# The third batch's mix as seven half products, and an attention stage laid out call by call

## The reference, cut to what matters

```python
# four batches of x [512 rows, 512 columns]; context [512 rows, 256]
q = ctx @ Wq.T + bq;  k = ctx @ Wk.T + bk
attention = softmax(q @ k.T)                      # 512 x 512
x = x + tanh(g_xattn) * (layernorm(x) @ attention.T)   # "the mix", 512 x 512 x 512
h = layernorm(x)
up, gate = h @ ternary(W_up).T, h @ ternary(W_gate).T  # 2048 columns each
x = x + tanh(g_ffn) * ((silu(up) * gate) @ ternary(W_down).T)
# ternary(w) = clip(round(w / scale), -1, 1) * scale, scale = mean(|w|)
```

## Time and profile before

| What | Value |
|---|---|
| median of three runs | 391.25 us |
| the profiled execution | 390.47 us |
| its span, first to last instruction | 388.6 us |
| tensor engine busy | 384.4 us, 99% of the span |
| VectorE, ScalarE, POOL busy | 315.8, 271.0, 196.5 us |
| attention stage on the tensor engine | until 91.28 us |
| granted clock | 1.00 in each of 40 slices |

### The profile page before, as it was taken

How to read it: one execution, slowest core, us unless ns; L and a number is a source line. 1 busy time by engine, 2 the same in 40 slices (tenths; PEclk the granted TensorE clock), 3 DMA queues, 4 the chain that set the end, 5 groups by cost and what they waited for, 6 DMA issues and landing times.

```text
span 388.6 us, 6367 instructions
## 1 busy us (share of the span) xinstructions
PE 384.4 (99%) x2043; PEld 223.9 (58%) x2048; DVE 315.8 (81%) x495; ACT 271.0 (70%) x372; POOL 196.5 (51%) x211
## 2 busy tenths in 40 slices
PE   8999999999999999999999999999999999999997
PEld 6676765554444444444444467556555665656886
DVE  0778897997898988879788987799787767769984
ACT  3887988899897898798887864583647455466300
POOL 0498727768783170586777533372736243444000
PEclk9999999999999999999999999999999999999999
DMA  8999987789600020300327820060006000000014
GB/s 282 401 402 408 408 263 189 176 267 182 163 2 1 13 96 0 110 1 0 110 51 131 147 54 3 0 215 3 2 1 218 0 2 0 2 0 3 0 64 153
DMA packets 44048, 43.92 MB, mean 113 GB/s; under 512 B 30832, under 2 KB 33008, under 8 KB 42992
## 3 DMA queue, kind: packets, MB, share of 16 engines
q1 hardware_dynamic: 44016, 43.53, 36.6%
HBM read 29.89 MB, written 6.29 MB: 93 GB/s over the span
## 4 chain that ended last, share of the span: by engine, by line
PE 98%; DMA 1%; DVE 0%; issue 0%; DVEq 0%
PE pair L1007 25%; PE pair L1005 25%; PE pair L1108 19%; PE pair L896 7%; PE pair L1079 7%; PE pair L919 6%; PE pair L869 4%; PE pair L853 3%; PE pair L880 2%; DMA xf<-in_first 1%; PE pair L934 1%; PE pair L938 0%; DVE x_sb L2148 0%; PE pair L926 0%; DVEq L404 0%
## 5 line engine op out<-in xcount | busy, mean ns | idle before, releaser
L1005 PE MATMUL pair<-xb_hi,w_sb 128*128 128x512 f16 x448 | 169.8, 379 | 0.0
L1007 PE MATMUL pair<-xb_lo,w_sb 128*128 128x512 f16 x448 | 169.8, 379 | 0.0
L1005 PEld LDWEIGHTS pair<-xb_hi,w_sb 128*128 128x128 fp8e4 x448 | 43.8, 98 | 50.0 <-issue 0.5
L1007 PEld LDWEIGHTS pair<-xb_lo,w_sb 128*128 128x128 fp8e4 x448 | 43.8, 98 | 49.8 <-issue 0.3
L2148 DVE SCALAR_TENSOR_TENSOR x_sb<-pair,small,x_sb 128x256 f32<-128x256 f32 (+1 forms) x85 | 38.7, 475 | 13.6 <-PE pair L1108 13.2
L1525 ACT ACTIVATE xf<-xf,small 128x512 f32<-128x512 f32 x48 | 34.2, 717 | 20.2 <-DVE xf L2096 9.6
L2101 DVE SCALAR_TENSOR_TENSOR xf<-xf,small 128x512 f32<-128x512 f32 x48 | 39.1, 822 | 2.5 <-ACT xf L1525 2.4
L2106 DVE TENSOR_TENSOR sh<-xf,sh 128x512 f16<-128x512 f32 x32 | 28.3, 889 | 1.5 <-ACT sh L1540 1.5
L2086 DVE TENSOR_TENSOR xf<-pair,xf 128x1024 f32<-128x1024 f32 x16 | 19.5, 1218 | 11.8 <-issue 8.4
L896 PE MATMUL pair<-sh,xt_sb 128*128 128x512 f32 (+2 forms) x80 | 28.6, 508 | 0.0
L1540 ACT ACTIVATE sh<-xf 128x512 f16<-128x512 f32 x32 | 19.8, 622 | 12.4 <-DVE xf L2101 12.4
(11 more groups left out here) (207 smaller groups left out, 788.9 us busy)
## 6 DMA issues: line engine op xcount, KB each, us to landing
w_sb<-in_wugT SPq DMA_DIRECT2D x8, 1024.0 KB, 15.5
x_sb<-in_x SPq DMA_DIRECT2D x4, 1024.0 KB, 13.4
xf<-in_wdT SPq DMA_DIRECT2D x4, 1024.0 KB, 8.0
xt_sb<-in_wdT SPq DMA_DIRECT2D x4, 1024.0 KB, 4.8
xt_sb<-in_xT SPq DMA_DIRECT2D x12, 256.0 KB, 6.0
x_dram<-x_sb SPq DMA_DIRECT2D x8, 256.0 KB, 3.5
out<-x_sb SPq DMA_DIRECT2D x8, 256.0 KB, 3.0
x_sb<-x_dram SPq DMA_DIRECT2D x4, 512.0 KB, 4.0
```

The costliest lines, as they stand in the source:

```text
L1005: pe.matmul(dst[:, m * 512:(m + 1) * 512], w[:, o:o + P], hi[:, k], start=start and k == 0, stop=False, skip_group_check=not start)
L1007: last = pe.matmul(dst[:, m * 512:(m + 1) * 512], w[:, o:o + P], lo[:, k], start=False, stop=k == 1, skip_group_check=not start)
```

## The change

Batch 2's mix is computed as seven products of halves as well. `NM = 3` batches go that way, where `NS = 2` did. Eight sums on POOL and fourteen pieces of addition on VectorE take the place of four direct tiles and four additions. The sums lie in blocks of `xb_hi` and `xb_lo` that are not yet filled (x sums in T2 and T3 and in `c21`, P sums in T1 and B22); their later owners get a wait for the products that read them. The loads of batch 3's input tiles now wait for batch 2's x sums and for product 2 (tiles 0 and 1) or 4 (tiles 2 and 3), since they reuse the same room, and all four stand ahead of block T3 on SyncE. Batch 1's and batch 2's normalizations are moved later, batch 2's behind the first expert product's addition. The loops of the attention stage are replaced on all engines by a list of single calls in another order. The first expert products stand between the last direct mixes of batch 3.

```diff
-    NS = 2
+    NM = 3
...
         def x_sum(b, k):
 
+            if b == 2:
+                home = (xb_block(0, "T2").bitcast(F32), xb_block(1, "T2").bitcast(F32), c21, xb_block(1, "T3").bitcast(F32))[k]
+                return home[:, 0:512].rearrange("p (i s) -> p i s", i=2)
             home = xf[:, 6144:8192] if b == 0 else xb_hi[:, 1024:5120].bitcast(F32)
             return home[:, k * 512:(k + 1) * 512].rearrange("p (i s) -> p i s", i=2)
 
...
         def p_sum(b, k):
 
+            if b == 2:
+                return xb_block(k // 2, ("T1", "B22")[k % 2]).bitcast(F32).rearrange("p (k m) -> p k m", k=2)
             o = b * 2048 + (0, 1024, 1536, 512)[k]
             return xf[:, o:o + 512].rearrange("p (k m) -> p k m", k=2)
...
                 if b == 2:
                     sp.wait_ge(s_mp, 7)
                 elif b == 3:
-                    sp.wait_ge(s_xm, i + 1)
+                    sp.wait_ge(s_ss, 12)
+                    sp.wait_ge(s_mp, mixed(2, 2 if i < 2 else 4))
                 sp.dma_start(xt_tile(b, i), xT[b, i]).then_inc(xt_in(b, i)[0], 16)
...
             def spill(g):
-                sp.wait_ge(s_x1, g - NS * NT + 1)
+                if g < NM * NT:
+                    sp.wait_ge(s_xe, added(2, 3 if g % NT < 2 else 4))
+                else:
+                    sp.wait_ge(s_x1, g - NM * NT + 1)
                 sp.dma_start(x1_dram[g // NT - 2, g % NT], x_tile(g // NT, g % NT)).then_inc(d_spill, 16)
...
+                if n == 0 and blk in ("T3", "T1", "B22"):
+                    sp.wait_ge(s_mp, mixed(2, {"T3": 3, "T1": 7, "B22": 4}[blk]))
...
             transpose_block(0, "B11")
             load_down(2)
             transpose_block(0, "B21")
-            load_xt(3, 0)
-            spill(8)
-            load_xt(3, 1)
-            spill(9)
+            for i in range(NT):
+                load_xt(3, i)
             transpose_block(0, "T3")
-            load_xt(3, 2)
             load_down(3)
+            for g in range(8, 10):
+                spill(g)
+            transpose_block(0, "T1")
             spill(10)
-            transpose_block(0, "T1")
-            load_xt(3, 3)
             spill(11)
             spill(12)
             transpose_block(0, "T2")
...
             def x_sum_1(b):
+                if b == 2:
+                    pool.wait_ge(s_mp, mixed(1, 3))
                 for i in range(NT):
                     pool.wait_ge(*xt_in(b, i))
                 pool.tensor_tensor(x_sum(b, 0), x_quarter(b, 1, 0), x_quarter(b, 1, 1), ALU.add).then_inc(s_ss, 1)
 
             def x_sum_2(b):
+                if b == 2:
+                    pool.wait_ge(s_mp, mixed(1, 4))
+                if b == 0:
+                    pool.wait_ge(s_pn0, NT - 1)
                 hold(pool, s_ss, 4 * b + 1)
                 pool.tensor_tensor(x_sum(b, 1), x_sum(b, 0), x_quarter(b, 0, 0), ALU.subtract).then_inc(s_ss, 1)
...
             def x_sum_4(b):
+                if b == 2:
+                    pool.wait_ge(s_abs, 2 * NABS)
                 hold(pool, s_ss, 4 * b + 2)
                 pool.tensor_tensor(x_sum(b, 3), x_quarter(b, 0, 1), x_sum(b, 1), ALU.subtract).then_inc(s_ss, 1)
...
             rstd2_two(0, 1)
-            rstd1(2, 0)
-            rstd1(2, 1)
+            rstd1_two(2, 0)
+            x_sum_1(2)
+            x_sum_2(2)
+            x_sum_3(2)
+            x_sum_4(2)
+            p_sum_1(2)
             rstd2_two(1, 0)
+            p_sum_2(2)
+            rstd1_two(2, 1)
             rstd2_two(1, 1)
-            hold(pool, s_x2n, 2 * NT)
-            pool.tensor_tensor(t3_sb, xf_half(1, 1), xf_half(1, 0), ALU.subtract).then_inc(s_t3, 1)
-            hold(pool, s_t3, 1)
-            pool.tensor_tensor(xf_half(1, 0), xf_half(1, 0), xf_half(0, 0), ALU.subtract).then_inc(s_t1, 1)
...
+            p_sum_3(2)
+            p_sum_4(2)
+            first_t3()
+            first_t1()
+            rstd1(3, 0)
+            rstd1(3, 1)
...
+            project(3, 0)
+            project(3, 1)
+            transpose_p(2, 3)
+            mix_product(2, 1)
+            energy(3, 0)
+            energy(3, 1)
+            mix_product(2, 2)
+            mix_product(2, 6)
+            energy(3, 2)
+            mix_product(2, 5)
+            transpose_p(3, 0)
+            mix_product(2, 7)
+            transpose_p(3, 1)
+            energy(3, 3)
+            mix_product(2, 3)
+            mix_product(2, 4)
+            transpose_p(3, 2)
+            transpose_p(3, 3)
+            mix(3, 0)
+            mix(3, 1)
             product1(0)
+            mix(3, 2)
             product2(0)
...
-            def add_mixed(b, j):
+            def add_mixed(b, j, i):
 
                 lh, mh = MIX_TO[j]
-                hold(dve, s_r1, b * NT + 2 * lh + 2)
-                for i in range(2):
-                    if j in MIX_BEFORE:
-                        hold(dve, s_xe, added(b, MIX_BEFORE[j]))
-                    cols = x_tile(b, 2 * lh + i)[:, mh * 256:(mh + 1) * 256]
-                    dve.wait_ge(s_mp, mixed(b, j))
-                    dve.scalar_tensor_tensor(cols, mix_bank(j)[:, i * 256:(i + 1) * 256], tr1_of(b, 2 * lh + i), cols,
-                                             ALU.mult, ALU.add).then_inc(s_xe, 1)
+                if i == 0:
+                    hold(dve, s_r1, b * NT + 2 * lh + 2)
+                if j in MIX_BEFORE:
+                    hold(dve, s_xe, added(b, MIX_BEFORE[j]))
+                cols = x_tile(b, 2 * lh + i)[:, mh * 256:(mh + 1) * 256]
+                dve.wait_ge(s_mp, mixed(b, j))
+                dve.scalar_tensor_tensor(cols, mix_bank(j)[:, i * 256:(i + 1) * 256], tr1_of(b, 2 * lh + i), cols,
+                                         ALU.mult, ALU.add).then_inc(s_xe, 1)
 
             def stats2(b, i):
-                if b < NS:
+                if b < NM:
                     hold(dve, s_xe, added(b, 3 if i < 2 else 4))
...
```

More of the change, by code:

```diff
@@ L175, in gated_block_kernel @@
         TARGET = {1: (0, 0), 2: (0, 0), 3: (0, 1), 4: (1, 0), 5: (1, 1), 6: (0, 1), 7: (1, 1)}
+        FIRST = {"B11": (0, 0), "B21": (0, 1), "T1": (1, 0), "T2": (0, 0), "B22": (1, 1), "T4": (0, 1)}
         def t_done(n, blk):
@@ L588, in rstd2_two @@
             def rstd2_two(b, h):
-                two, own = slice(2 * h, 2 * h + 2), slice(b * NT + 2 * h, b * NT + 2 * h + 2)
+                two, own = slice(2 * h, 2 * h + 2), slice(b % 2 * NT + 2 * h, b % 2 * NT + 2 * h + 2)
                 hold(pool, s_ln2, b * NT + 2 * h + 2)
@@ new lines, in _ @@
+            norm_p(1, 0)
+            norm_p(1, 1)
+            sum_abs(0, 1)
+            sum_abs(0, 2)
+            copy_at(1, 0)
+            exp_row(1, 2)
+            norm_p(1, 2)
+            copy_at(1, 1)
+            exp_row(1, 3)
+            copy_at(1, 2)
+            norm_p(1, 3)
+            sum_abs(0, 3)
+            copy_at(1, 3)
+            bias_qk(2, 0)
+            bias_qk(2, 1)
+            sum_abs(1, 0)
+            sum_abs(1, 1)
+            exp_row(2, 0)
+            sum_abs(1, 2)
@@ new lines, in _ @@
+            exp_row(2, 1)
+            norm_p(2, 0)
+            sum_abs(1, 3)
+            norm_p(2, 1)
+            exp_row(2, 2)
+            copy_at(2, 0)
+            norm_p(2, 2)
+            block_high(0, "B11")
+            sum_abs(2, 0)
+            copy_at(2, 1)
+            exp_row(2, 3)
+            copy_at(2, 2)
+            block_high(0, "B21")
+            norm_p(2, 3)
+            bias_qk(3, 0)
+            copy_at(2, 3)
+            bias_qk(3, 1)
+            sum_abs(2, 1)
+            round_part(0, 0)
@@ L2080, in _, with weights_up, weights_down, first_t2 @@
-            hold(dve, s_t4, 1)
-            low_t(0, "T4", xf_half(0, 1))
+                stats1(0, i)
+                aggregate1(0, i)
+            def weights_up():
+                weight_scale(0, 2, ps_q, 0)
+            def weights_down():
+                weight_scale(2, 3, ps_pt[0], 3)
+            def first_t2():
+                hold(dve, s_t1, 1)
+                hold(dve, s_tl, t_done(0, "B11"))
+                dve.tensor_tensor(xf_half(0, 0), t3_sb, xf_half(0, 0), ALU.add).then_inc(s_t2, 1)
@@ new lines, in _ @@
+            add_mixed(1, 4, 0)
+            stats1(2, 2)
+            row_rsum(2, 3)
+            aggregate2(1, 0)
+            first_low("B11")
+            add_mixed(1, 4, 1)
+            stats2(1, 2)
+            aggregate1(2, 2)
+            first_low("B21")
+            aggregate2(1, 1)
+            stats2(1, 3)
+            aggregate2(1, 2)
+            stats1(2, 3)
+            aggregate1(2, 3)
+            add_mixed(2, 1, 0)
+            add_mixed(2, 1, 1)
+            row_max(3, 0)
+            aggregate2(1, 3)
```

708 lines of the change are left out of this document (363 added, 345 removed).

## The result

The kernel before has a median of 390.88 us (390.22 to 391.39), the changed kernel 394.37 us (392.05 to 394.86), nine runs each. The ratio of the means (393.9 and 390.9) is 1.0076, 95% interval 1.0055 to 1.0097; the medians differ by 3.5 us, 0.9%. The change makes the kernel slower by 0.8%. The forecast was 393.5 us in a range of 389.4 to 395.3.

The account below looks back on a forecast made before the run. The tensor engine, busy 384.4 of 388.6 us, was taken as the bound, so every new wait is lost outright. Waits of 3.1 + 0.4 + 0.5 + 0.4 less 1.7 saved gave +2.7 on 390.8: 393.5 us, range 389.4 to 395.3.

Parts of the forecast that it names:

- likeliest case: Attention stage, batch 2: POOL's sums come late, with collisions; +2.7 us, 393.5 us, by itself 392.2 to 394.8; chance 0.46.
- main term: Tensor engine at batch 2's product 6: waits 3.1 us for POOL's second P sum, 1.5 us without collisions.
- collision: POOL's x sums of batch 2 beside VectorE's B11 and B21 subtractions: two collisions at 0.8 us each.
- saved work: Tensor engine, batch 2's stretch: 18.96 us before, 17.3 us after, 1.7 us saved.
- Product 7: Batch 2, tensor engine: waits 0.4 us for POOL's third P sum, 5.0 us plus a semaphore against 4.8 of cover.
- Product 3: Batch 2, tensor engine: waits for product 5's VectorE additions behind batch 1's four normalizations; 0.5 us, between 0 and 1.8.
- Mix 0: Batch 3's first direct mix: waits 0.4 us for transpose 2's copy and the last product's addition.
- Rival 3: Tensor engine's clock falls in the 3 us wait: +1.5 to +2 us, 395.3 us; chance 0.05.
- Rival 1: Batch 2's POOL sums made in time, only mix 0's wait left: -1.3 us, 389.5 us; chance 0.21.
- Rival 2: Batch 2's POOL sums late but without collision with VectorE's subtractions: +1.1 us, 391.9 us; chance 0.22.
- Rival 4: ScalarE's high part of T2, behind T3's transposes, delays the second unit's first product: +1.5 us, 395.0 us; chance 0.06.
- SyncE's queue behind T3 had cover: Transfers behind T3's transposes costed at nothing; without cover, 1 to 2 us added before the second expert product.

Follow-up runs that it names:

- experiment 1: Changed kernel with batch 2's four transposed input tiles loaded right behind its x tiles: 390.3 us, ratio 0.9981 to the kernel before (repeat 390.2 us, 0.9986).
- experiment 2: Kernel before with only the load order edited, batch 2's four transposed tiles right behind its x tiles: 391.2 us, ratio 1.0004.
- experiment 6: Changed kernel with early tiles, POOL's second P sum of batch 2 made three times and partly once more: 395.67 us, ratio 1.0109 to the kernel before.
- experiment 3: Changed kernel with POOL making P sums 1 and 2 right behind x sums 1 and 2: 392.39 us, ratio 1.0036 to the kernel before.
- experiment 8: As experiment 7, but VectorE makes T3's low part ahead of product 4's additions and batch 2's statistics: 389.66 us, ratio 0.9963 to the kernel before.
- experiment 5: Changed kernel with twelve constant matmuls, result unread, ahead of product 6: 392.81 us, ratio 1.0044 to the kernel before.
- experiment 4: Changed kernel with VectorE's subtractions B11 and B21 moved later, past the x sums: 396.52 us, ratio 1.014 to the kernel before.
- experiment 7: Changed kernel with early tiles, direct mixes in the other PSUM bank, transpose 2 ahead of product 4, its additions ahead of batch 2's statistics: 391.15 us, ratio 1.0006.

## Why the prediction was right

**The likeliest case came about, and its main term was right.** The tile was there at about 56.0 (forecast 55.8), the first two x sums collided, and product 6 waited 3.06 us against 3.1. That the total came so near the measured time is in part luck, as shown below: the sum was about 1 us too large, and a fall of the clock that it left out made up for it. Experiments 1, 2 and 6 show the cause by taking the wait away and putting it back.

**Its steps were each off a little, in the same direction.** POOL's second P sum ended at 66.69 against 66.5 by my sum, and product 6's place in a full row was at 63.6 against 63.5. Inside that, a collision cost 0.95 and 0.99 us, not 0.8. The x sums began 0.14 and 0.08 us behind the subtractions' starts, which then had 1.09 and 1.12 us to run; in my row of before the sum began 0.22 behind, 1.00 us were left, and it cost 0.85. All three cost what is left of the subtraction, less about 0.14. The Trainium skill (SBUF — State Buffer, "SBUF: two separate sides") has the pair of ports locked for the whole instruction, the other engine fully blocked: the three rows agree with that. Experiment 3 adds a fourth (L619 at 56.90, 1.17 us left, 1.03 paid). I had read 0.85 as a weaker mechanism, when it was the same one with a later start.

**The saved work was smaller**: 1.34 us in experiment 8's stretch, where no wait stands, and 1.5 in the changed kernel, against 1.7 by seven products at 1.73. Some products take up to 0.1 us more than the 1.73 spacing (in the changed kernel the product at 66.83 is followed after 1.81, the one at 74.74 after 1.83), and these small steps add up. In experiment 5, where the first of these has its input ready 0.9 us early, the same two are followed after 1.73: so it is not the products themselves but, it seems, an input that comes at the last moment.

**Terms that were too large.** Product 7: forecast 0.4, measured 0. Product 3: forecast 0.5, measured 0.06. Mix 0: forecast 0.4, measured 0.42. Product 7's term was mis-sized: both sides of it start at the end of the second P sum, and POOL's rstd of two tiles took 2.24 us (66.77 to 69.01), not the 2.6 of the one row that I read, which has an idle 0.5 us inside. With 1.0 and 1.27 behind it the third P sum ended 4.6 us after the second, inside the 4.8 of cover; I had 5.0. Product 3's 0.5 was an allowance between 0 and 1.8: the four normalizations took 2.93 us together, and the additions ended at 74.68, the moment of product 3's place. What such a chain costs depends on where the tensor engine is: in experiment 3, with the wait at product 6 gone, POOL's factors came at the same time as before and product 3 waited 1.45 us. (The 1.43 at product 7 in experiment 4 has another cause, the moved collisions.)

In all, waits of 3.2 (66.83 against a place at 63.61), 0.06 and 0.42 less 1.5 of saved work (20.73 us from 58.43 to 79.16, less the first two waits, against 18.96) make 2.2 us; with a start 0.1 later these are the 2.3 of the profile. The full-clock runs' mean is 1.6 above the 390.9 of before. The forecast was 2.7.

**Rival 3 was undervalued.** I gave the falling clock 0.05, and as an alternative to the likeliest case. It came on top of it, in six of nine runs, and cost 2.0 us there (394.5 against 392.5), as I had priced it (1.5 to 2). The median lies in that group. So 393.5 lies between the two groups, and 0.9 below the median: a sum some 1 us too large stood in for half of a clock fall of 2.0, which is luck. I argued that no idle stretch of that size was followed by matmuls in the trace of before; that was no evidence against it, since there was none to look at. What does bear on it is the Trainium skill (TensorE: Matmul & The Clock Gate, "Part 1: The HAM clock gate"): idleness takes the array back to half clock. The windows of experiment 4 agree, 0.50 after the wait, and 5 and 6 agree on both sides.

**Rival 1** (sums in time, 389.5) is what experiment 1 made real: 390.3, 0.8 above my number, with the wait of 0.2 to 0.4 at mix 0 as written. **Rival 2** was not tried cleanly, since the way to miss the collision cost more elsewhere; on POOL's side its number held, a second P sum at 65.13 in experiment 4 against 64.9. **Rival 4** (ScalarE's later chain) did not come in the changed kernel. A neighbour of it did in experiment 7: I had written that SyncE's queue behind T3 had cover, and 1 to 2 us to lose before the second expert product if that went. It went with 0.9 us of VectorE delay, and cost 1.5.

**Open.** The times of experiments 3 and 4 are each about 1 us more than their waits and, in 4, the slow-clock stretch explain; late openings were in both profiles (first product of batch 0 at 17.75 and 18.91, against 16.72 before), and whether in all their runs is not known. The openings of the profiled runs differ by up to 2.4 us (first product of batch 0 between 16.5 and 18.9), and before two profiles are compared they have to be lined up there. Why three of nine runs kept the clock is not shown, nor how long the wait was in the six that lost it: the profile is of a run that kept it. That the fall in those six came right behind product 6 is inferred from experiments 1, 5 and 6.

## What to carry to other kernels

Where one engine has no idle time, rewriting its work saves only if every new input is there early: trace each new operand back to its load, and move that load in the same edit (here 0.8% slower without, 0.2% faster with it, for the same arithmetic). Price a wait in front of the tensor engine at its length plus what a fallen clock costs behind it. When you move a late job, look for who reads it next; in experiments 3, 4 and 7 the wait reappeared one or more steps on, in 4 and 7 by way of a DMA queue in which other transfers stood behind the delayed one.

## What the hardware showed that I had not expected

- A tensor engine that was otherwise busy throughout lost its clock with a single long wait behind the opening: in six of nine runs where the profile has 3.06 us, in three of four where it has 3.6, and in all four of the kernel with waits of 1.4, 0.6 and 2.05 us close together. With a longest wait of 1.45 us it fell in none of ten runs, with one of 1.51 (experiment 7) in none of twelve, and with matmuls filling the wait in none of ten. The one profile that shows the stretch at 1.2 GHz has it for a bit over 3 us and loses 1.7 us of time; the groups of runs lie 2.0 and 2.7 us apart.
- The profiled run of the changed kernel was one without the fall, so it shows 2.3 of the 3.5 us by which the medians differ. The granted clocks of all runs had to be read beside it.
- A POOL sum of 1.27 us took 2.2 to 2.3 beside one VectorE subtraction of 1.2 us over two SBUF tensors, and VectorE, where it came second, paid instead: 1.82 for 1.2 in experiment 8, behind a POOL sum that had 0.7 us to run. Small operations pay as well: one of 0.19 us took 1.27 beside such a subtraction (experiment 4).
